# A graph network on one core: low halves unscaled and summed into the high halves' 256 PSUM columns

## The chip, the cores and the metric

The kernel runs on one core of one Trainium2 chip. Its time is the device time of one execution in microseconds (us). The engines are TensorE (PE; its weight loads are listed as PEld), VectorE (DVE), ScalarE (ACT), GpSimd (POOL) and SyncE (SP), which issues most transfers. Each runs its own instruction stream in order, and they meet at semaphores.

## What is computed

A graph of 3125 nodes with 256 features and 50000 edges goes through three layers of three hops each; then comes a residual sum and a layer norm. In short:

```python
norm = dis[src] * dis[dst]              # dis = 1/sqrt(in-degree)
def _tagconv(x, src, dst, norm, W, b):
    out = x @ W[0]
    h = x
    for k in range(1, 4):
        h = segment_sum(norm[:, None] * h[src], dst)
        out = out + h @ W[k]
    return out + b
h = relu(_tagconv(x, ..., W1, b1))
h = relu(_tagconv(h, ..., W2, b2))
out = layernorm(x + _tagconv(h, ..., W3, b3))
```

## The kernel before

**The work.** With g = sqrt(degree) * h and A the matrix of edge counts, a layer is evaluated from its last weight inwards: V3 = (g W3)/degree, V2 = (g W2 + A V3)/degree, V1 = (g W1 + A V2)/degree, and the layer's result is g W0 + A V1. Nodes lie in 25 tiles of 128 (NT = 25; the last has 53 real rows). The items of the program are `("P", L, k, t)`, the product of layer L, weight k and node tile t, and `("T", L, t)`, the transpose of g's tile t into `gT`. `schedule()` writes their order: k = 3 for all 25 tiles, then k = 2, 1, 0, with the transposes and the k = 3 products of layer L+1 placed between the k = 0 tiles of layer L, two tiles behind. The last of them (tile 23, the transpose of 24, tile 24) are placed inside the first k = 2 tile of the next layer, after 3, 10 and 15 of its neighbour products (WQ, WT, WP). Each "P" with k < 3 is called a hop tile here.

**Two halves.** float32 values are held as two float16 numbers, a high half and a low half. `Whl`, `gT` and `V` keep both. The low half is the remainder times SC = 2048, so it needs a sum of its own: a 128x512 PSUM bank holds the high sum in columns 0 to 255 and the scaled low sum in columns 256 to 511. A tile's own product takes two 512-column matmuls of gT's high half against both halves of the weights (L683) and two 256-column matmuls of gT's low half (L685). The neighbour sum takes 24 matmuls of 512 columns, one per source tile, with A's fp8 counts as stationary operand and both halves of V moving (L703), and one of 256 columns for the last source tile, whose 64 rows of high and 64 of low halves share 128 partitions (L708). Its stationary operand `AT` is a float16 copy of those counts, divided by SC in the lower 64 partitions; POOL makes it (L508, L510).

**How a hop tile ends.** For k > 0 four operations alternate between two engines: ACT copies the low columns times 1/degree to `t1` (L597), DVE adds the high columns times SC/degree and writes the sum back to PSUM (L930), ACT rounds it to float16 as the new high half in `V` (L578), DVE subtracts that from PSUM and writes the low half (L908). For k = 0 ACT makes `t1`, DVE makes bias plus `t1` (L935), adds the high columns (L937) and takes the maximum with zero (L941); in the last layer L948, L950 and L954 take the place of these and the layer norm follows. `TensorE` may write a PSUM bank again when DVE has finished with its former tile; five banks rotate (`emptied`).

**The beginning.** About 37 us build degrees, edge lists and the first columns of A. A itself is built from one-hot matrices (DVE L808 and L810, PE L624, ACT L554) in groups, the rest of them inside the first hop stage (L = 0, k = 2), where `trailing()` orders DVE's and ACT's work on groups and on finished tiles. Chained DVE operations on the degrees make the columns of `cst` (L828 to L839), and POOL's scaling of x (L503) waits for the last of them. `largest()` keeps maxima for a check of ranges; if any of 15 lies outside LOW to HIGH, a slow general path runs at the end.

## Time and profile before

| | |
|---|---|
| median of 3 runs | 1498.56 us (1498.47 to 1499.02) |
| the profiled execution: its own time | 1500.34 us |
| its span, first to last instruction | 1498.1 us |
| PE busy, matmuls | 1456.0 us, x7741 |
| DVE busy | 677.7 us, x1608 |
| ACT busy | 360.3 us, x850 |
| POOL busy | 64.0 us, x146 |

The profiled execution lasts 2.2 us longer than its span, and 1.8 us longer than the median of the runs. Busy times are unions, so matmuls that overlap in the array count once. The times of the stages, from the chain of waits: k = 3 of the first layer from about 42 to 71 us, the first hop stage with A's construction to 243 us, and then hop stages of 25 tiles each.

### The profile page before, as it was taken

How to read it: one execution, taken by the hardware profiler on the slowest of the kernel's cores; microseconds unless marked ns; L12 is line 12 of the kernel's file. 1: busy time of each engine (PE TensorE's matmuls, PEld its weight loads, DVE VectorE, ACT ScalarE, POOL GpSimd, SP SyncE). 2: the span in 40 equal slices, each digit the busy share in tenths (PEclk: the TensorE clock that was granted, in tenths of full speed). 3: DMA queues.
4: the chain of work that ended last, by engine and by line, in shares of the span. 5: the costliest groups of instructions: out<-in, count | busy, mean ns of one | idle time of the engine just before them, and what ended most of it. 6: DMA issues, size and time to landing. Idle time of an engine off the chain costs nothing.

```text
span 1498.1 us, 18986 instructions
## 1 busy us (share of the span) xinstructions
PE 1456.0 (97%) x7741; PEld 730.1 (49%) x7741; DVE 677.7 (45%) x1608; ACT 360.3 (24%) x850; POOL 64.0 (4%) x146
## 2 busy tenths in 40 slices
PE   3999999999999999999999999999999999999996
PEld 2555555444455554444444445554444444444443
DVE  7866663333344444333533334445333333335554
ACT  5766663111122222111111112222111111111110
POOL 3300000221000000000000000000000000000000
PEclk9999999999999999999999999999999999999998
DMA  2200000000000000000000000000000000001110
GB/s 72 87 1 1 2 1 1 24 23 11 1 1 1 1 1 0 1 1 1 0 0 1 1 1 1 1 0 1 1 1 0 1 0 1 1 6 48 43 43 22
DMA packets 15470, 15.11 MB, mean 10 GB/s; under 512 B 2362, under 2 KB 15218, under 8 KB 15378
## 3 DMA queue, kind: packets, MB, share of 16 engines
q1 hardware_dynamic: 15138, 13.18, 2.9%
q8 instruction: 63, 1.03, 0.3%
q0 software_dynamic: 240, 0.66, 0.2%
q14 instruction: 29, 0.24, 0.1%
HBM read 10.62 MB, written 3.21 MB: 9 GB/s over the span
## 4 chain that ended last, share of the span: by engine, by line
PE 95%; DVE 4%; issue 1%; ACT 0%; POOL 0%; DMA 0%; DVEq 0%; ACTq 0%
PE pb L703 77%; PE pb L683 8%; PE pb L685 4%; PE pb L624 2%; PE pb L708 2%; PE pb L665 1%; DVE pb L930 1%; DVE V L908 1%; DVE gT L889 0%; PE pb L635 0%; PE pb L646 0%; POOL g L503 0%; DVE Whl L808 0%; DVE Whl L810 0%; ACT t L597 0%
## 5 line engine op out<-in xcount | busy, mean ns | idle before, releaser
L703 PE MATMUL pb<-V,A 128*128 128x512 f16 x5400 | 1226.8, 379 | 0.0
L703 PEld LDWEIGHTS pb<-V,A 128*128 128x128 fp8e4 x5400 | 522.1, 98 | 580.9
L930 DVE SCALAR_TENSOR_TENSOR pb<-pb,cst,t 128x256 f32<-128x256 f32 x225 | 110.2, 490 | 467.3 <-ACT t L597 467.3
L597 ACT ACTIVATE t<-pb,cst 128x256 f32<-128x256 f32 x250 | 118.6, 474 | 691.5 <-PE pb L708 673.7
L683 PE MATMUL pb<-Whl,gT 128*128 128x512 f16 x600 | 210.8, 382 | 0.7 <-DVE gT L889 0.5
L685 PE MATMUL pb<-Whl,gT 128*128 128x256 f16 x600 | 164.6, 274 | 0.0
L908 DVE SCALAR_TENSOR_TENSOR V<-V,pb 128x256 f16<-128x256 f16 (+1 forms) x225 | 94.4, 420 | 92.0 <-ACT V L578 91.8
L578 ACT ACTIVATE V<-pb 128x256 f16<-128x256 f32 (+1 forms) x225 | 86.0, 382 | 140.2 <-DVE pb L930 140.2
L554 ACT ACTIVATE A<-pb 128x500 fp8e4<-128x500 f32 (+1 forms) x157 | 91.3, 585 | 41.7 <-PE pb L624 41.3
L935 DVE SCALAR_TENSOR_TENSOR w<-bb,cst,t 128x256 f32<-128x256 f32 x50 | 24.2, 484 | 168.6 <-ACT t L597 168.6
L921 DVE TENSOR_REDUCE ast<-A 128x1 f32<-128x800 uint8 x100 | 97.6, 976 | 0.0
L683 PEld LDWEIGHTS pb<-Whl,gT 128*128 128x128 f16 x600 | 59.1, 99 | 65.4 <-issue 3.8
L847 DVE TENSOR_REDUCE stat<-V 128x1 f32<-128x256 f16 x225 | 90.7, 412 | 0.3
L624 PE MATMUL pb<-Whl 128*128 128x125 f16 x625 | 63.5, 226 | 6.2 <-ACT A L554 3.7
L624 PEld LDWEIGHTS pb<-Whl 128*128 128x128 f16 x625 | 49.4, 100 | 39.9 <-ACT A L554 6.8
L597 ACT ACTIVATE t<-pb 128x256 f32<-128x256 f32 x50 | 19.2, 384 | 191.5 <-PE pb L708 191.5
L685 PEld LDWEIGHTS pb<-Whl,gT 128*128 128x128 f16 x600 | 59.1, 99 | 7.2
L708 PE MATMUL pb<-V,AT 128*128 128x256 f16 x225 | 61.5, 273 | 0.0
L808 DVE TENSOR_TENSOR Whl<-Whl 128x1024 f16<-128x1024 f16 x79 | 54.2, 686 | 1.4
L810 DVE TENSOR_TENSOR Whl<-Whl 128x1000 f16<-128x1000 f16 x79 | 53.0, 671 | 0.0
L950 DVE SCALAR_TENSOR_TENSOR w<-pb,cst,t 128x256 f32<-128x256 f32 x25 | 12.1, 483 | 55.5 <-ACT t L597 55.5
L708 PEld LDWEIGHTS pb<-V,AT 128*128 128x128 f16 x225 | 22.1, 98 | 27.2 <-DVE V L908 1.0
(118 smaller groups left out, 397.3 us busy)
## 6 DMA issues: line engine op xcount, KB each, us to landing
xr<-in_x SPq DMA_DIRECT2D x48, 128.0 KB, 2.1
out<-g SPq DMA_DIRECT2D x24, 128.0 KB, 1.7
xr<-in_W SPq DMA_DIRECT2D x16, 128.0 KB, 2.0
V<-in_W SPq DMA_DIRECT2D x2, 512.0 KB, 4.1
bb<-in_b SPq DMA_DIRECT2D x3, 128.0 KB, 4.9
xr<-in_x SPq DMA_DIRECT2D x2, 53.0 KB
gT<-in_table,idx POOLq DMA_INDIRECT x5, 2.7
out<-g SPq DMA_DIRECT2D x1, 53.0 KB
```

The costliest lines, as they stand in the source:

```text
L554: act.activation(A8[:, :, gi * GW:gi * GW + n * GD].rearrange("p a (g w) -> p a g w", w=GD), BB[gi % 2][:, 0:n * KEYS].rearrange("p (g a w ...
L578: act.activation(V[vbuf[(L, k)]][0:r, t, 0:F], PB[e][0:r, 0:F], ACT.Copy, scale=1.0 / SC).then_inc(S["s_a2"], 1)
L597: act.activation(t1[:, e % RB, :], lo, ACT.Copy, scale=sc).then_inc(S["s_a1"], 1)
L624: mm = pe.matmul(BB[gi % 2][:, k * KEYS:(k + 1) * KEYS], OB[:, b % NO, vis % BV // VL, :, vis % VL], OK[:, b % NO, vis % BV // VL, :, vis ...
L683: pe.matmul(acc[:, :], gT[:, t, c, 0, :], Whl[:, L, c, k, :], start=(c == 0), stop=False, skip_group_check=True)
L685: mm = pe.matmul(acc[:, F:512], gT[:, t, c, 1, :], Whl[:, L, c, k, 0:F], start=False, stop=(k == 3 and c == 1), skip_group_check=True)
L703: mm = pe.matmul(acc[:, :], A8[:, a, t * P:(t + 1) * P], src[:, a, :], start=False, stop=False, skip_group_check=True)
L708: mm = pe.matmul(acc[:, 0:F], AT[:, t * P:(t + 1) * P], src[:, a, 0:F], start=False, stop=True, skip_group_check=True)
L847: dve.tensor_reduce(stat[:, col:col + 1], ap, axis, ALU.max, apply_absolute_value=True).then_inc(S["s_st"], 1)
L908: dve.scalar_tensor_tensor(lo, vb[0:r, t, 0:F], -SC, hi[0:r, :], ALU.mult, ALU.add).then_inc(S["s_v"], 1)
L921: dve.tensor_reduce(ast[:, nam:nam + 1], A8[:, a_, 800 * i_:800 * i_ + 800].bitcast(U8), AX.X, ALU.max).then_inc(S["s_st"], 1)
L930: dve.scalar_tensor_tensor(hi, hi, cst[:, 1, t:t + 1], t1[:, e % RB, :], ALU.mult, ALU.add).then_inc(S["s_d1"], 1)
```

## The change

SC goes. Low halves are plain remainders (weights are now scaled by SV = 64 and g by SG = 16 in place of 16 and 1, which keeps the remainders away from float16's smallest numbers; LOW becomes 0.25). So all products can be added into the same 256 columns, and every 512-column matmul becomes two of 256 columns with the same stationary operand. A finished tile with k > 0 is read twice from PSUM: ACT writes the high half with the scale 1/degree, DVE writes the low half as PSUM times 1/degree minus the high half. For k = 0 DVE alone reads the sum; ACT's step is gone. The transposed g's low half is a plain subtraction. `AT` is gone: POOL copies the last source tile's counts into the unused 64 partitions of A8's last tile, one operation in place of two. The low halves of the weights of layers 2 and 3 come from one DVE operation each, where POOL made three. The columns of `cst` are 4, not 5, and a column's worth of SC multiplication is gone: two operations less in the chain on the degrees. The order on ACT and DVE has no separate second item ("V") any more.

```diff
-SC = 2048.0
-SV = 16.0
+SG = 16.0
+SV = 64.0
-LOW = 2.0 ** -10
+LOW = 0.25
...
-def trailing(sched, empty, split):
+def trailing(sched, empty):
...
+        t = it[3]
+        gs = [("B", gi) for gi in groups_of(t + 1)]
+        out += gs[:empty] + ([("P", 0, 2, t - 1)] if t else []) + gs[empty:]
+        if t == NT - 1:
+            out.append(it)
...
             for t in range(NT):
                 pool.wait_ge(S["s_ev"], groups_of(t)[-1] + 1)
-                src = A8[0:HALF, NT - 1, t * P:(t + 1) * P]
-                pool.tensor_copy(AT[0:HALF, t * P:(t + 1) * P], src).then_inc(S["s_at"], 1)
-                pool.wait_ge(S["s_at"], 2 * t + 1)
-                pool.tensor_scalar(AT[HALF:P, t * P:(t + 1) * P], AT[0:HALF, t * P:(t + 1) * P], 1.0 / SC, 0.0, ALU.mult,
-                                   ALU.add).then_inc(S["s_at"], 1)
...
+                pool.wait_ge(*((S["s_at"], t) if t else (S["s_gx"], NT)))
+                pool.tensor_copy(A8[HALF:P, NT - 1, t * P:(t + 1) * P],
+                                 A8[0:HALF, NT - 1, t * P:(t + 1) * P]).then_inc(S["s_at"], 1)
...
-            act.wait_ge(S["s_whi"], 1)
-            act.activation(Wsc, hl[:, :, 0:F], ACT.Copy, scale=SC).then_inc(S["s_wp"], 1)
...
+                _, L, k, t = it
+                if k > 0:
+                    act.wait_ge(S["s_ps"], pe_no[(L, k, t)] + 1)
                     r = P if t < NT - 1 else HALF
-                    act.activation(V[vbuf[(L, k)]][0:r, t, 0:F], PB[e][0:r, 0:F], ACT.Copy,
-                                   scale=1.0 / SC).then_inc(S["s_a2"], 1)
+                    act.activation(V[vbuf[(L, k)]][0:r, t, 0:F], PB[pe_no[(L, k, t)]][0:r, 0:F], ACT.Copy,
+                                   scale=cst[0:r, 0, t:t + 1]).then_inc(S["s_a2"], 1)
...
-                act.activation(t1[:, e % RB, :], lo, ACT.Copy, scale=sc).then_inc(S["s_a1"], 1)
...
-                acc = PB[e]
+                acc = PB[e][:, 0:F]
                 for c in range(2):
-                    pe.matmul(acc[:, :], gT[:, t, c, 0, :], Whl[:, L, c, k, :], start=(c == 0), stop=False,
-                              skip_group_check=True)
-                    mm = pe.matmul(acc[:, F:512], gT[:, t, c, 1, :], Whl[:, L, c, k, 0:F], start=False,
+                    for h in range(2):
+                        pe.matmul(acc, gT[:, t, c, 0, :], Whl[:, L, c, k, F * h:F * h + F], start=(c + h == 0), stop=False,
+                                  skip_group_check=True)
+                    mm = pe.matmul(acc, gT[:, t, c, 1, :], Whl[:, L, c, k, 0:F], start=False,
                                    stop=(k == 3 and c == 1), skip_group_check=True)
...
-                            mm = pe.matmul(acc[:, :], A8[:, a, t * P:(t + 1) * P], src[:, a, :], start=False,
-                                           stop=False, skip_group_check=True)
+                            for h in range(2):
+                                pe.matmul(acc, A8[:, a, t * P:(t + 1) * P], src[:, a, F * h:F * h + F], start=False,
+                                          stop=False, skip_group_check=True)
...
-            dl_(dve.tensor_scalar(cst[:, 1, :], cst[:, 0, :], SC, None, ALU.mult))
...
-            dl_(dve.tensor_scalar(cst[:, 3, :], dg[:, 5, :], 2.0 / SV, None, ALU.mult))
-            dve.tensor_scalar(cst[:, 4, :], dg[:, 5, :], 2.0 / (SV * SC), None, ALU.mult).then_inc(S["s_cs"], 1)
+            dve.tensor_scalar(cst[:, 3, :], dg[:, 5, :], 2.0 / (SV * SG), None, ALU.mult).then_inc(S["s_cs"], 1)
...
-                    dve.scalar_tensor_tensor(lo, vb[0:r, t, 0:F], -SC, hi[0:r, :], ALU.mult,
-                                             ALU.add).then_inc(S["s_v"], 1)
+                    dve.scalar_tensor_tensor(lo, acc[0:r, :], cst[0:r, 0, t:t + 1], vb[0:r, t, 0:F], ALU.mult,
+                                             ALU.subtract).then_inc(S["s_v"], 1)
+                    if (L, k) == (0, 2):
+                        largest(v_no[(0, 3, t)], V[vbuf[(0, 3)]][:, t, 0:F], AX.X)
...
-                    dve.wait_ge(S["s_a1"], e + 1)
-                    dve.scalar_tensor_tensor(hi, hi, cst[:, 1, t:t + 1], t1[:, e % RB, :], ALU.mult,
-                                             ALU.add).then_inc(S["s_d1"], 1)
...
+                    dve.tensor_scalar(t2[:, t % 2, :], bb[:, L, :], cst[:, 2, t:t + 1], None,
+                                      ALU.mult).then_inc(S["s_z"], 1)
+                    dve.wait_ge(S["s_z"], L * NT + t + 1)
+                    dve.wait_ge(S["s_ps"], e + 1)
+                    dve.scalar_tensor_tensor(we, acc, 1.0 / SV, t2[:, t % 2, :], ALU.mult,
+                                             ALU.add).then_inc(S["s_d1"], 1)
...
+                    dve.wait_ge(S["s_z"], 2 * NT + t + 1)
+                    dve.wait_ge(S["s_ps"], e + 1)
+                    dve.scalar_tensor_tensor(we, acc, cst[:, 3, t:t + 1], t2[:, t % 2, :], ALU.mult,
                                              ALU.add).then_inc(S["s_d1"], 1)
...
-                    dl_(dve.tensor_tensor(we, we, t2[:, t % 2, :], ALU.add))
```

One hop tile on TensorE, in program order, before the change: the tile's own product, the 24 neighbour matmuls and the last source tile.

```order
L683 MATMUL pb<-Whl,gT 128x512
L685 MATMUL pb<-Whl,gT 128x256
L683 MATMUL pb<-Whl,gT 128x512
L685 MATMUL pb<-Whl,gT 128x256
L703 MATMUL pb<-V,A 128x512 x24
L708 MATMUL pb<-V,AT 128x256
```

The same hop tile in the changed kernel, where L639, L641, L660 and L665 are the lines of L683, L685, L703 and L708.

```order
L639 MATMUL pb<-Whl,gT 128x256 x2
L641 MATMUL pb<-Whl,gT 128x256
L639 MATMUL pb<-Whl,gT 128x256 x2
L641 MATMUL pb<-Whl,gT 128x256
L660 MATMUL pb<-V,A 128x256 x48
L665 MATMUL pb<-V,A 128x256
```

The order of the items on TensorE is as it was; 26 instructions of 512 columns have become 52 of 256.

DVE at the turn from layer L to layer L+1, before the change: the last k = 0 tile (L935, L937, L941), the transposed tile 23 (L889), the k = 3 tiles 22 and 23, and the transposed tile 24.

```order
L935 SCALAR_TENSOR_TENSOR w<-bb,cst,t 128x256
L937 SCALAR_TENSOR_TENSOR w<-pb,w 128x256
L941 TENSOR_SCALAR g<-w 128x256
L889 SCALAR_TENSOR_TENSOR gT<-gT,pb 128x2x128
L847 TENSOR_REDUCE stat<-gT 128x1
L930 SCALAR_TENSOR_TENSOR pb<-pb,cst,t 128x256
L908 SCALAR_TENSOR_TENSOR V<-V,pb 128x256
L847 TENSOR_REDUCE stat<-V 128x1
L930 SCALAR_TENSOR_TENSOR pb<-pb,cst,t 128x256
L908 SCALAR_TENSOR_TENSOR V<-V,pb 128x256
L847 TENSOR_REDUCE stat<-V 128x1
L889 SCALAR_TENSOR_TENSOR gT<-gT,pb 128x2x128
```

DVE at the same place in the changed kernel (L888, L892 and L896 are the k = 0 tile, L844 the transposed tile, L861 the low half, L802 the maxima).

```order
L888 TENSOR_SCALAR w<-bb,cst 128x256
L892 SCALAR_TENSOR_TENSOR w<-pb,w 128x256
L896 TENSOR_SCALAR g<-w 128x256
L844 TENSOR_TENSOR gT<-pb,gT 128x2x128
L802 TENSOR_REDUCE stat<-gT 128x1
L861 SCALAR_TENSOR_TENSOR V<-pb,cst,V 128x256
L802 TENSOR_REDUCE stat<-V 128x1
L861 SCALAR_TENSOR_TENSOR V<-pb,cst,V 128x256
L802 TENSOR_REDUCE stat<-V 128x1
L844 TENSOR_TENSOR gT<-pb,gT 128x2x128
```

Each k = 3 tile has one operation less here and no pause between its two, and L888 no longer needs the tile's sum, so it stands ahead of the wait for TensorE.

## Rows read from the trace of the kernel before

**Rows 1.** The page: busy time by engine, and the chain that ended last.

```profile
PE 1456.0 (97%) x7741; PEld 730.1 (49%) x7741; DVE 677.7 (45%) x1608; ACT 360.3 (24%) x850; POOL 64.0 (4%) x146
...
PE 95%; DVE 4%; issue 1%; ACT 0%; POOL 0%; DMA 0%; DVEq 0%; ACTq 0%
```

**Rows 2.** The chain: start us, length us, what; bodies of hop tiles.

```profile
247.82 5.18 PE pb L703 x24
...
402.24 5.18 PE pb L703 x24
...
421.14 5.18 PE pb L703 x24
...
564.10 5.18 PE pb L703 x24
```

**Rows 3.** Timeline of PE near 480 us: start us, us, engine, line.

```profile
480.62 0.27 PE L708 MATMUL pb<-V,AT 128*128 128x256 f16 x1
480.73 0.38 PE L665 MATMUL pb<-identf,g 128*128 128x128 f32 x2
480.95 0.38 PE L683 MATMUL pb<-Whl,gT 128*128 128x512 f16 x1
```

**Rows 4.** The page's groups: xcount | busy us, mean ns of one | idle before.

```profile
L703 PE MATMUL pb<-V,A 128*128 128x512 f16 x5400 | 1226.8, 379 | 0.0
L703 PEld LDWEIGHTS pb<-V,A 128*128 128x128 fp8e4 x5400 | 522.1, 98 | 580.9
L930 DVE SCALAR_TENSOR_TENSOR pb<-pb,cst,t 128x256 f32<-128x256 f32 x225 | 110.2, 490 | 467.3 <-ACT t L597 467.3
```

**Rows 5.** The chain at the end of the degree work, DVE.

```profile
35.68 0.19 DVE cst L831
...
37.45 0.19 DVE cst L839
```

**Rows 6.** Timeline of PE, last k = 3 tiles of the first layer.

```profile
68.32 0.38 PE L703 MATMUL pb<-V,A 128*128 128x512 f16 x1
...
68.81 0.39 PE L683 MATMUL pb<-Whl,gT 128*128 128x512 f16 x1
...
69.47 0.38 PE L703 MATMUL pb<-V,A 128*128 128x512 f16 x1
...
69.90 0.39 PE L683 MATMUL pb<-Whl,gT 128*128 128x512 f16 x1
```

**Rows 7.** Timeline after the first layer's last k = 3 tile.

```profile
70.76 0.48 ACT L597 ACTIVATE t<-pb,cst 128x256 f32<-128x256 f32 x1 [0.34 <-PE pb L685]
...
72.65 0.69 DVE L808 TENSOR_TENSOR Whl<-Whl 128x1024 f16<-128x1024 f16 x1
...
74.08 0.58 PE L624 MATMUL pb<-Whl 128*128 128x125 f16 x4 [0.96 <-DVE Whl L810]
...
74.46 0.63 PE L703 MATMUL pb<-V,A 128*128 128x512 f16 x1
```

**Rows 8.** Busy us (xcount) of PE, PEld, DVE, ACT, POOL, then granted clock.

```profile
74.00:77.40 3.40, 3.32 (x19) 2.11 (x20) 3.40 (x6) 2.13 (x4) 0.73 (x1) 0.52 0.00 0
```

**Rows 9.** The chain: bodies of hop tiles around the two turns of layers.

```profile
579.14 5.18 PE pb L703 x24
...
1032.02 5.18 PE pb L703 x24
1047.07 5.18 PE pb L703 x24
```

**Rows 10.** The chain after TensorE's last matmul.

```profile
1486.40 0.48 ACT t L597
...
1486.91 0.49 DVE w L950
...
1487.43 0.43 DVE w L954
...
1487.89 0.44 DVE lnb L956
```

More of the change, by code:

```diff
@@ L287, in groups_of @@
     return list(range(last[t] + 1, last[t + 1] + 1)) if t < NT else []
-def trailing(sched, empty, split):
+def trailing(sched, empty):
     out = []
-    held = None
     for it in sched:
-        if it[0] == "T":
+        if it[0] == "T" or it[1:3] != (0, 2):
             out.append(it)
             continue
-        L, k, t = it[1:]
-        if k == 2 and held:
-            out.append(held)
-            held = None
-        if (L, k) == (0, 2):
-            gs = [("B", gi) for gi in groups_of(t + 1)]
-            before = ("P", 0, 2, t - 1), ("V", 0, 2, t - 1)
-            out += (gs[:empty] + ([before[0]] if t else []) + gs[empty:split] + ([before[1]] if t else [])
-                    + gs[split:])
-            if t == NT - 1:
-                out += [it, ("V",) + it[1:]]
-            continue
-        out.append(it)
-        if held:
-            out.append(held)
-        held = ("V",) + it[1:] if k > 0 else None
-        if held and (L, k) != (0, 3):
-            out.append(held)
-            held = None
+        t = it[3]
[3 more added lines that the diff above has]
+            out.append(it)
     return out
@@ L333, in bass_tag_gnn_layernorm @@
     p_of = {e: key for key, e in pe_no.items()}
+    d_no = {key: n for n, key in enumerate(key for key in pe_no if key[1] == 0)}
     vbuf = {(L, k): (L + 3 - k) % 2 for L in range(3) for k in (3, 2, 1)}
@@ L560, in _ @@
             act.wait_ge(S["s_cs"], 1)
-            for it in trailing(SCHED, 0, 2):
+            for it in trailing(SCHED, 0):
                 if it[0] == "B":
@@ L569, in _ @@
                     act.activation(gT[:, t, :, 0, :], TB[j % 2][:, 0:F].rearrange("p (c m) -> p c m", c=2),
-                                   ACT.Copy, scale=1.0 / SC).then_inc(S["s_th"], 1)
+                                   ACT.Copy).then_inc(S["s_th"], 1)
                     continue
-                what, L, k, t = it
-                e = pe_no[(L, k, t)]
-                if what == "V":
-                    v = v_no[(L, k, t)]
-                    act.wait_ge(S["s_d1"], e + 1)
+                _, L, k, t = it
+                if k > 0:
+                    act.wait_ge(S["s_ps"], pe_no[(L, k, t)] + 1)
                     r = P if t < NT - 1 else HALF
-                    act.activation(V[vbuf[(L, k)]][0:r, t, 0:F], PB[e][0:r, 0:F], ACT.Copy,
-                                   scale=1.0 / SC).then_inc(S["s_a2"], 1)
+                    act.activation(V[vbuf[(L, k)]][0:r, t, 0:F], PB[pe_no[(L, k, t)]][0:r, 0:F], ACT.Copy,
+                                   scale=cst[0:r, 0, t:t + 1]).then_inc(S["s_a2"], 1)
                     if (L, k) == (0, 1) and t < 16:
@@ L585, in _ @@
                                        scale=SV).then_inc(S["s_wi"], 1)
[L586 to L598 removed]
+                elif L == 2:
                     act.wait_ge(S["s_ln"], t + 1)
@@ L611, in emptied @@
                 else:
-                    pe.wait_ge(S["s_d1"], pe_no[was] + 1)
+                    pe.wait_ge(S["s_d1"], d_no[was] + 1)
             def build(gi):
@@ L651, in _ @@
                 build(gi)
-            pe.wait_ge(S["s_wp"], 2)
+            pe.wait_ge(S["s_wp"], 1)
             def work(it, within={}):
@@ L702, in work @@
                         if a < NT - 1:
-                            mm = pe.matmul(acc[:, :], A8[:, a, t * P:(t + 1) * P], src[:, a, :], start=False,
-                                           stop=False, skip_group_check=True)
+                            for h in range(2):
+                                pe.matmul(acc, A8[:, a, t * P:(t + 1) * P], src[:, a, F * h:F * h + F], start=False,
+                                          stop=False, skip_group_check=True)
                             continue
                         if (L, k) == (0, 2):
-                            pe.wait_ge(S["s_at"], 2 * t + 2)
-                        mm = pe.matmul(acc[:, 0:F], AT[:, t * P:(t + 1) * P], src[:, a, 0:F], start=False,
+                            pe.wait_ge(S["s_at"], t + 1)
+                        mm = pe.matmul(acc, A8[:, a, t * P:(t + 1) * P], src[:, a, 0:F], start=False,
                                        stop=True, skip_group_check=True)
@@ L879, in verdict_ranges @@
                                   ALU.mult).then_inc(S["s_ck"], 1)
-            for it in trailing(SCHED, 4, 6):
+            for it in trailing(SCHED, 4):
                 if it[0] == "B":
@@ L894, in _ @@
                     continue
-                what, L, k, t = it
+                _, L, k, t = it
                 e = pe_no[(L, k, t)]
-                hi = PB[e][:, 0:F]
+                acc = PB[e][:, 0:F]
                 we = w[:, t % 2, :]
@@ L901, in _ @@
                     vb = V[vbuf[(L, k)]]
-                if what == "V":
                     dve.wait_ge(S["s_a2"], v + 1)
```

68 lines of the change are left out of this document (20 added, 48 removed).

## The prediction

> **What bounds the kernel now.** I read the page first: PE is busy for 97% of the span and makes up 95% of the chain that ended last, DVE and ACT are busy 45% and 24% [rows 1]. So the question is what a hop tile's stream of matmuls costs, and at which few places TensorE waits for the ends of tiles. The chain in order of time shows how regular the stream is. In the plain hop stages one tile body follows the next from 247.82 to 402.24 us, 26 tiles apart, which is 5.939 us a tile; in the k = 0 stages that carry transposes and k = 3 products as well, 21 tiles lie between 421.14 and 564.10 us, 6.808 us each [rows 2]. No wait stands between them. A DVE or ACT operation saved inside these stages buys nothing; what TensorE itself does there counts in full.
>
> From these two periods follows the price of one matmul, start to start. Call it x for 512 columns and y for 256. A plain tile is 26x + 3y (24 L703 and two L683; two L685 and one L708). The richer tile adds two transposes and one more product, 2 transposes + 2x + 2y = 6.808 - 5.939 = 0.868 us. Two transposes take 0.22 us, as much as two 256-column matmuls [rows 3], so 2x + 4y = 0.868. Solved: x = 215.8 ns, y = 109.2 ns. The check is the body itself, 24x = 5.18 us [rows 2]. The mean of 379 ns in the page's group is the time from start to result of one matmul, most of it overlapped, and must not be used as its price [rows 4].
>
> **What the change adds.** A pair of 256-column matmuls costs 2y = 218.4 ns where one of 512 cost 215.8: 2.5 ns more, a fixed part paid once more. Pairs: 5400 for L703 [rows 4] and 600 for L683 (300 products, two each), 6000 in all. 6000 x 2.53 ns = 15.1 us, in every stage, all of it on TensorE, which has no slack. From the rounding of the rows the pair's price is good to 0.1 ns, 0.6 us in the sum.
>
> This takes a step that no row shows: a 256-column matmul behind another 256-column one with the same weights. The weight load takes 98 ns [rows 4] and must fit into a slot of 109. In the trace a load does hide in such a slot once per L708 and L685, with a 512-column matmul next; now it must do so 55 times in a row. Bounds: if nothing extra is paid for the second matmul, 0; if the fixed part is paid, 15; if the load does not hide, much more (the second rival). I take 15.1, since y was measured with a load in its slot.
>
> **What it saves.** Only the places where TensorE waits for a tile's end.
> - Degrees: two of the chained DVE operations go, each about 0.2 us with its hand-over, and POOL and TensorE wait behind the last [rows 5]: -0.4 us.
> - The last k = 3 tiles of the first layer: TensorE stands from 68.32 + 0.216 to 68.81 and from 69.47 + 0.216 to 69.90 [rows 6], 0.27 and 0.21 us, because DVE with three operations a tile frees banks late. With two operations DVE has slack (its own period was the same 1.08 us as TensorE's): -0.5 us.
> - After them, DVE starts the one-hots for which TensorE waits until 74.08 only when the last tile is finished: 72.65 - 70.76 = 1.89 us of four operations in turn [rows 7]. Now two: ACT's with a column as scale, like L597, 0.48 us, and DVE's at L930's 0.49 [rows 4], with hand-overs 1.02 us. -0.9 us.
> - Right behind, from 74.0 to 77.4 us, the granted clock is 0.52, the lower level of 1.2 GHz [rows 8], after TensorE had mostly stood for some three microseconds; a 512-column matmul then takes 0.63 us [rows 7]. With 3.32 us of matmuls in it, that costs up to 1.66 us. Since the waits ahead of it shrink by a third or more, it may not happen. Ends 0 and -1.6; I take -0.8.
> - The two turns of layers. Between the bodies at 564.10 and 579.14 stand 58 matmuls of x and 16 of y (two k = 3 products inside the tile and one before it, the transposes): 14.27 us, where 15.04 passed; at the second turn 15.05 (1032.02 to 1047.07) [rows 2, 9]. TensorE stands 0.78 us each time, for transposed tiles and V tiles that DVE delivers late. There DVE loses about 0.9 us on the k = 0 tile (ACT's step and L935 are out of the way) and some 0.8 on each of the k = 3 tiles 22 and 23, far more than the waits. -1.6 us. What would be late next is the k = 3 tile 24 behind its transpose; by my count its low half of gT comes about 0.1 us ahead of need.
> - The end: from 1486.40 to 1487.89 run ACT, L950 and L954 [rows 10], 1.49 us; one DVE operation of 0.49 remains. -1.0 us.
>
> Edits at no cost: POOL's one copy for two operations and no weight work; one more DVE operation of some 0.42 us in 16 tiles of the first layer's k = 1 stage and the moved maxima (DVE is below half busy there, under a 6 us tile); ACT's first-layer weight pass, done long before TensorE reads weights. If that cover went, each would cost its own length, under 0.5 us a tile. Nothing is queued behind the new waits for TensorE on DVE that was not behind the wait for ACT before: L888 now even stands ahead.
>
> **Sum.** +15.1 - 0.4 - 0.5 - 0.9 - 0.8 - 1.6 - 1.0 = +9.9 us. On the profiled execution, 1500.3 us (span 1498.1 and 2.2 around it), that gives 1510.2; the median of the runs is 1.8 lower, so **1508.5 us**. With the savings between 4.4 and 6.0 and the pairs at 15.1 +- 0.6 the case spans 1507.0 to 1509.9.
>
> **The rivals.**
> - *The pair costs nothing more: faster.* If the second matmul of a pair, whose weights are already there, follows the first without the fixed part, x stands for a pair and only the savings remain: 1498.6 - 5.2 = 1493.4 us. It decides from below 0.35 ns a pair on ((5.2 - 3.0)/6000); up to 1.4 ns a pair it would look like no change. For it: the weights do repeat. Against: the fixed part is the same 2.5 ns for 128 float32 columns, 256 and 512 (x - 2y), so it hangs on the matmul and not on new weights. 5%.
> - *Weight loads or sums into columns written 109 ns before become the bound: much slower.* A load of 98 ns leaves 11 ns. If the slot became 98 + 20, say, 55 slots a tile would cost 0.5 us each, 110 us over 225 tiles; every 1 ns is 12 us. Against: y itself holds a load, and L685 adds into columns that the L683 ahead of it wrote some 109 ns earlier, at no visible cost. 7%.
> - The Trainium skill, "TensorE: Matmul & The Clock Gate", section "Back-to-back issue gap", speaks against halving: it gives sustained streams of load and matmul 81 ns at 128 columns and 131 ns at 512, a large fixed part for each pair. Read between these, 256 columns would take some 98 ns, a pair 196 for 131, an estimate of 6000 x 65 ns = 390 us more. Here the trace disagrees: 512 columns take 215.8 ns, not 131. It is this rival's far end, and I leave it 1 of the 7%.
> - *The savings don't come: +15.* A new order lets another operation be late (transposed tile 24 above all), or the lower clock comes at another place, or the two-operation ends are not on the chain where I think. Price: 5 us, 1513.7; with a second stretch of lower clock 1515. 8%.
>
> **How the numbers follow.** Forecast 77%, its near neighbours 3% (a pair price between 0.35 and 1.4 ns, which ends as no change), rivals 5, 7 and 8%. A change of 0.2% is 3.0 us, about what a measurement of this kernel can tell. Faster 0.05, same 0.03, slower 0.92. The range reaches from 1504 (a pair at 1.8 ns) to 1514 (no savings), and leaves out some 15%.
>
> **What would show it.** In the changed profile: 13,741 matmuls; the plain tile's body, now 48 matmuls, 5.24 us, and the tile period 55y = 6.00 us (+0.065); bodies at the turns 14.4 us apart; no wait of TensorE on DVE after the k = 3 stage's banks; the last matmul's end followed by one DVE operation before the layer norm; DVE's busy time down by some 100 us and ACT's by some 120, at no gain of their own. It would be wrong if the period of the plain stages stayed at 5.94, or rose beyond 6.05 us.

## The result and the profile after

The changed kernel takes **1510.82 us**, the median of 3 runs (1510.66 to 1511.25), where the kernel before took 1498.56: 12.3 us more, a ratio of 1.0082 (95% interval 1.0059 to 1.0104). Its profiled execution took 1510.66 us, with a span of 1508.9.

The page of the changed kernel, with the lines that answer to [rows 1] and [rows 4]. L660 is the old L703, L861 the DVE operation that is left of L930 and L908, L545 the ACT operation that is left of L597 and L578.

```profile
PE 1467.7 (97%) x13741; PEld 1316.0 (87%) x13741; DVE 569.1 (38%) x1372; ACT 253.1 (17%) x549; POOL 34.1 (2%) x73
...
PE 97%; DVE 2%; issue 1%; POOL 0%; DMA 0%; ACT 0%; DVEq 0%; ACTq 0%
...
L660 PE MATMUL pb<-V,A 128*128 128x256 f16 x10800 | 1239.9, 273 | 0.0
L660 PEld LDWEIGHTS pb<-V,A 128*128 128x128 fp8e4 x10800 | 1050.2, 98 | 119.3
L861 DVE SCALAR_TENSOR_TENSOR V<-pb,cst,V 128x256 f16<-128x256 f32 (+1 forms) x225 | 108.4, 482 | 603.8 <-ACT V L545 603.7
L545 ACT ACTIVATE V<-pb,cst 128x256 f16<-128x256 f32 (+1 forms) x225 | 106.7, 474 | 741.2 <-PE pb L665 714.6
```

6000 matmuls have come, 13,741 in place of 7,741, and each brings a weight load with it (730 us of loads have become 1316). DVE works 109 us less and ACT 107 us less, but DVE's share of the chain that ended last only falls from 4% to 2%. That is the whole trade: a little more on the engine that bounds the kernel, a lot less on two that do not.

The chain of the changed kernel (start us, length us, what), which answers to [rows 2] and [rows 9]: the first and last of 27 bodies in the plain stages, and the bodies on either side of the first turn of layers.

```profile
11.69 7.96 issue
247.72 5.24 PE pb L660 x48
...
403.83 5.24 PE pb L660 x48
...
567.36 5.24 PE pb L660 x48
581.87 5.24 PE pb L660 x48
```

26 tiles lie between 247.72 and 403.83: 6.004 us each, where 5.939 stood. That is 0.065 us for 26 pairs, **2.50 ns a pair**; 6000 pairs are 15.0 us. The turn takes 14.51 us in place of 15.04. The first row is one that I had not looked at: a stretch of 7.96 us in the prologue was 6.11 before. The timelines of both kernels there, first before (start, length, engine and line, in brackets how long the engine had waited and for whom):

```profile
12.18 1.18 POOL L496 DMA_INDIRECT gT<-in_table,idx  x1 [6.06 <-DVE idx L745]
12.61 2.29 DVE L749 SCALAR_TENSOR_TENSOR Whl<-V 128x2048 f16<-128x2048 f32 x1 [0.73 <-ACT V L535]
13.67 2.06 POOL L496 DMA_INDIRECT gT<-in_table,idx  x1 [0.30 <-issue]
15.26 0.29 DVE L770 TENSOR_TENSOR g<-gT,thr 128x128 f32<-128x128 int32 x1 [0.36 <-DMA gT<-in_table,idx]
```

And after:

```profile
11.81 2.29 DVE L706 SCALAR_TENSOR_TENSOR Whl<-V,Whl 128x2048 f16<-128x2048 f32 x1
12.19 2.96 POOL L478 DMA_INDIRECT gT<-in_table,idx  x1 [6.06 <-DVE idx L702]
15.46 0.95 POOL L478 DMA_INDIRECT gT<-in_table,idx  x1 [0.30 <-issue]
...
17.07 0.29 DVE L727 TENSOR_TENSOR g<-gT,thr 128x128 f32<-128x128 int32 x1 [2.97 <-DMA gT<-in_table,idx]
```

DVE makes the first layer's low halves in one operation of 2.29 us. Before, it had to wait 0.73 us for ACT's pass (L535), and POOL began the first gather's issue 0.43 us ahead of it and had it done in 1.18 us; the second issue, which began beside the DVE operation, took 2.06 and ended 0.83 us after it. The change removes ACT's pass; DVE starts at 11.81, ahead of the gather, and now the first issue takes 2.96 us and ends 1.05 us after DVE does. The table's first rows reach DVE at 17.07 instead of 15.26, **1.8 us later**, and the whole prologue moves with them.

The places where TensorE waited, in the changed kernel. The first stage's end, which answers to [rows 6] and [rows 7]:

```profile
70.95 0.38 PE L660 MATMUL pb<-V,A 128*128 128x256 f16 x2
71.16 0.47 ACT L545 ACTIVATE V<-pb,cst 64x256 f16<-64x256 f32 x1 [0.40 <-PE pb L641]
...
71.66 0.48 DVE L861 SCALAR_TENSOR_TENSOR V<-pb,cst,V 64x256 f16<-64x256 f32 x1 [0.39 <-ACT V L545]
72.17 0.69 DVE L765 TENSOR_TENSOR Whl<-Whl 128x1024 f16<-128x1024 f16 x1
...
74.78 0.40 PE L579 MATMUL pb<-Whl 128*128 128x125 f16 x4 [0.35 <-DVE Whl L767]
```

From ACT's start to DVE's one-hots 1.01 us pass, where 1.89 did. The half-speed stretch is not there; the windows' row for the stretch of [rows 8] says (the figure before the 0.03 is the granted clock):

```profile
74.00:77.40 3.40, 3.05 (x36) 2.69 (x35) 3.40 (x8) 2.67 (x6) 1.30 (x1) 1.00 0.03 5
```

At the turn, DVE's transposed tile 24 (L844) and the product that needs it:

```profile
577.13 1.26 PE L660 MATMUL pb<-V,A 128*128 128x256 f16 x10
577.75 0.42 DVE L844 TENSOR_TENSOR gT<-pb,gT 128x256 f16<-128x256 f32 x1 [0.84 <-ACT gT L538]
...
578.32 0.38 PE L639 MATMUL pb<-Whl,gT 128*128 128x256 f16 x2
```

Ten matmuls at 109.1 ns from 577.13 end at 578.22; L639 starts at 578.32. By this TensorE still stands 0.10 us at each turn.

The end, which answers to [rows 10]:

```profile
1498.31 0.48 DVE L906 SCALAR_TENSOR_TENSOR w<-pb,cst,w 128x256 f32<-128x256 f32 x1 [2.79 <-PE pb L665]
1498.83 0.43 DVE L910 BATCH_NORM_STATS2 lnb<-w 128x6 f32<-128x256 f32 x1
```

0.52 us where 1.49 stood.

**Where the 10.8 us between the two spans are** (1498.1 to 1508.9), in us:

| place | predicted | found | from |
|---|---|---|---|
| 6000 pairs | +15.1 | +15.0 | tile period 5.939 to 6.004 |
| gather behind DVE | not priced | +1.8 | first data at 15.26, now 17.07 |
| degrees | -0.4 | -0.4 | two operations gone: 3.08 us of chain, now 2.67 |
| last k = 3 tiles of the first stage | -0.5 | -1.1 | bank waits 0.49; the rest below |
| one-hots behind them | -0.9 | -0.9 | 1.89 to 1.01 |
| half-speed stretch | -0.8 | -1.0 | granted clock 0.52, now 1.00; a wait of 0.35 that comes with full speed taken off |
| two turns | -1.6 | -1.4 | TensorE stood 0.78 us at each, now 0.10 |
| end | -1.0 | -1.0 | 1.49 to 0.52 |
| sum | +9.9 | +11.0 | |

The places come to 0.2 us more than the spans differ; I could not place that. The rest in the fourth line is an estimate. In both traces a lone 256-column matmul is recorded at 0.42 us until about 46.6 us and at 0.27 from there on, as at half speed and at full speed, though the views give the granted clock as 1.00 on both sides. TensorE starts its products 1.4 us later in the changed kernel, so fewer of them are slow ones. The same delay is thus a loss in the prologue and a small gain behind it. The size of that gain is an accident of the two executions: over the eleven traces of this case the matmuls become short anywhere between 44.7 and 47.9 us, and each us of that is worth about half a us. Nor does the table say that the half-speed stretch went because of the change; experiment 7 has a trace on that.

### The profile page after: what moved, and what is told of

Same layout as the page of the kernel before. It is cut to its first block, busy times and chain, and to the rows that moved or that the text cites. A ratio compares the mean times of both kernels' runs of the same rounds, so it can differ in the third digit from the quotient of the medians.

```text
span 1508.9 us, 30155 instructions
## 1 busy us (share of the span) xinstructions
PE 1467.7 (97%) x13741; PEld 1316.0 (87%) x13741; DVE 569.1 (38%) x1372; ACT 253.1 (17%) x549; POOL 34.1 (2%) x73
## 2 busy tenths in 40 slices
DMA packets 15511, 15.83 MB, mean 10 GB/s; under 512 B 2362, under 2 KB 15218, under 8 KB 15378
## 4 chain that ended last, share of the span: by engine, by line
PE 97%; DVE 2%; issue 1%; POOL 0%; DMA 0%; ACT 0%; DVEq 0%; ACTq 0%
PE pb L660 78%; PE pb L639 9%; PE pb L641 4%; PE pb L579 2%; PE pb L665 2%; PE pb L620 1%; PE pb L590 0%; DVE Whl L765 0%; DVE Whl L767 0%; PE pb L601 0%; POOL g L485 0%; DVE V L731 0%; DVE V L700 0%; DMA t<-in_heads 0%; DVE t L696 0%
## 5 line engine op out<-in xcount | busy, mean ns | idle before, releaser
L660 PE MATMUL pb<-V,A 128*128 128x256 f16 x10800 | 1239.9, 273 | 0.0
L660 PEld LDWEIGHTS pb<-V,A 128*128 128x128 fp8e4 x10800 | 1050.2, 98 | 119.3
L861 DVE SCALAR_TENSOR_TENSOR V<-pb,cst,V 128x256 f16<-128x256 f32 (+1 forms) x225 | 108.4, 482 | 603.8 <-ACT V L545 603.7
L545 ACT ACTIVATE V<-pb,cst 128x256 f16<-128x256 f32 (+1 forms) x225 | 106.7, 474 | 741.2 <-PE pb L665 714.6
L639 PE MATMUL pb<-Whl,gT 128*128 128x256 f16 x1200 | 211.5, 274 | 0.0
L641 PE MATMUL pb<-Whl,gT 128*128 128x256 f16 x600 | 164.1, 274 | 0.0
L639 PEld LDWEIGHTS pb<-Whl,gT 128*128 128x128 f16 x1200 | 117.7, 98 | 13.5 <-issue 0.4
L892 DVE SCALAR_TENSOR_TENSOR w<-pb,w 128x256 f32<-128x256 f32 x50 | 21.2, 425 | 223.7 <-PE pb L665 223.7
L802 DVE TENSOR_REDUCE stat<-V 128x1 f32<-128x256 f16 x225 | 92.1, 409 | 0.3
L538 ACT ACTIVATE gT<-pb 128x256 f16<-128x256 f32 x75 | 28.8, 384 | 292.0 <-PE pb L620 292.0
L641 PEld LDWEIGHTS pb<-Whl,gT 128*128 128x128 f16 x600 | 58.9, 98 | 7.0
L665 PE MATMUL pb<-V,A 128*128 128x256 f16 x225 | 61.3, 273 | 0.0
L906 DVE SCALAR_TENSOR_TENSOR w<-pb,cst,w 128x256 f32<-128x256 f32 x25 | 12.1, 484 | 68.5 <-PE pb L665 68.5
L844 DVE TENSOR_TENSOR gT<-pb,gT 128x256 f16<-128x256 f32 x75 | 31.3, 418 | 3.2 <-ACT gT L538 3.2
L802 DVE TENSOR_REDUCE stat<-gT 128x1 f32<-128x256 f16 x75 | 30.7, 409 | 0.0
L620 PE MATMUL pb<-identf,g 128*128 128x128 f32 x150 | 29.9, 283 | 0.6 <-POOL g L485 0.6
```

Source lines behind the costliest of these rows:

```text
L545: act.activation(V[vbuf[(L, k)]][0:r, t, 0:F], PB[pe_no[(L, k, t)]][0:r, 0:F], ACT.Copy, scale=cst[0:r, 0, t:t + 1]).then_inc(S["s_a2"], 1)
L639: pe.matmul(acc, gT[:, t, c, 0, :], Whl[:, L, c, k, F * h:F * h + F], start=(c + h == 0), stop=False, skip_group_check=True)
L641: mm = pe.matmul(acc, gT[:, t, c, 1, :], Whl[:, L, c, k, 0:F], start=False, stop=(k == 3 and c == 1), skip_group_check=True)
L660: pe.matmul(acc, A8[:, a, t * P:(t + 1) * P], src[:, a, F * h:F * h + F], start=False, stop=False, skip_group_check=True)
L665: mm = pe.matmul(acc, A8[:, a, t * P:(t + 1) * P], src[:, a, 0:F], start=False, stop=True, skip_group_check=True)
L802: dve.tensor_reduce(stat[:, col:col + 1], ap, axis, ALU.max, apply_absolute_value=True).then_inc(S["s_st"], 1)
```

## The experiments

Each experiment was timed beside the kernel before on its own chip; the first four shared one chip (before: 1499.67 us, 7 runs, 1498.41 to 1500.69), the next four another (before: 1499.75, 16 runs, 1497.63 to 1501.77). The letters of the theories are those of the expectations: A is that every matmul has a fixed part of 2.5 ns, which halving pays a second time, and that the rest of the change only shows where TensorE waited.

### 1. Only the matmul cut in two, into separate halves

Into the kernel before. If summing into columns just written has a price (B), this has it not.

```
-                            mm = pe.matmul(acc[:, :], A8[:, a, t * P:(t + 1) * P], src[:, a, :], start=False,
-                                           stop=False, skip_group_check=True)
+                            for h in range(2):
+                                pe.matmul(acc[:, F * h:F * h + F], A8[:, a, t * P:(t + 1) * P],
+                                          src[:, a, F * h:F * h + F], start=False, stop=False, skip_group_check=True)
```

> The kernel before, with only the neighbour matmuls (L703) cut into two of 256 columns, the high half into columns 0 to 255 and the low half into 256 to 511; scales, ends of tiles and everything else as before. Theory A (a fixed part of 2.5 ns is paid for each matmul, whatever it writes): 5400 more matmuls, +13.5 us, 1512 us, and a plain tile period of 5.939 + 24 x 0.0025 = 6.000 us. Rival B (the cost comes from adding two matmuls in a row into the same 256 columns): no change, 1498.6 us, period 5.94.

Measured: 1511.73 us (1511.61 to 1512.47, 4 runs), ratio 1.0082 (1.0066 to 1.0099). The chain of this kernel, first and last of 27 bodies:

```profile
247.52 5.24 PE pb L704 x48
...
403.50 5.24 PE pb L704 x48
```

156 us for 26 tiles, 5.999 each: 0.060 us more for 24 pairs, 2.50 ns a pair, to separate columns as to the same. The cut alone, without the rescaling or the shorter ends, costs 12.1 us here; 5400 pairs at 2.5 ns are 13.5, which the interval (9.9 to 14.8 us) holds. B is out.

### 2. High halves first, then low halves

In the changed kernel, outside the first hop stage: the two matmuls that share their weights no longer follow each other.

```
+                    apart = (L, k) != (0, 2)
...
-                            for h in range(2):
+                            for h in range(1 if apart else 2):
                                 pe.matmul(acc, A8[:, a, t * P:(t + 1) * P], src[:, a, F * h:F * h + F], start=False,
                                           stop=False, skip_group_check=True)
                             continue
+                        for a2 in range(NT - 1 if apart else 0):
+                            pe.matmul(acc, A8[:, a2, t * P:(t + 1) * P], src[:, a2, F:512], start=False,
+                                      stop=False, skip_group_check=True)
```

> The changed kernel, with the 24 matmuls of the high halves first and then the 24 of the low halves in all hop stages but the first, so that neighbouring matmuls have different weights. Theory A (2.5 ns hang on the matmul): no change, 1510.8 us, period 6.00 us. Rival C (a repeated weight load makes the second matmul of a pair cheaper or dearer than one with new weights): the period moves; a cheaper repeat of 1 ns would show as +4.8 us (200 tiles x 24).

Measured: 1512.56 us (1511.79 to 1512.85, 4 runs), ratio 1.0085 (1.0068 to 1.0102). Its chain splits the body in its two halves:

```profile
430.11 2.62 PE pb L661 x24
432.73 2.62 PE pb L665 x24
```

Twice 2.62 is the same 5.24: whether the weights change from one matmul to the next or repeat makes no difference. The span grew by 2.0 us over the changed kernel's, and for another reason. The k = 3 products and transposes are placed after so many values of a; with one matmul per value ahead of them in place of two, they come earlier than DVE can deliver. In this kernel TensorE waits for the transposed tile 24 longer than 0.10 us:

```profile
577.52 0.38 PE L639 MATMUL pb<-Whl,gT 128*128 128x256 f16 x2 [0.48 <-DVE gT L848]
```

I count 0.9 us of standing per turn here, 1.6 us more at the two turns together; most of the other 0.4 lies where the matmuls become short, 0.7 us later in this execution. The place where prediction and trace put the next late operation is thus real: as soon as the need comes earlier, the wait there grows.

### 3. The first layer's ACT pass put back

To hold DVE's low-half operation back as before, for the 1.8 us of the prologue.

```
+            act.wait_ge(S["s_whi"], 1)
+            act.activation(Wsc, hl[:, :, 0:F], ACT.Copy, scale=1.0).then_inc(S["s_whi"], 1)
...
-            dve.wait_ge(S["s_whi"], 1)
+            dve.wait_ge(S["s_whi"], 2)
```

> The changed kernel, with the removed ACT pass over the first layer's weights put back (its result is not used) and DVE's low-half operation waiting for it as before, so that this operation of 2.29 us starts at about 12.6 us in place of 11.8. Theory D (it overlaps the work of GpSimd that issues the first gather, which took 2.96 us in place of 1.18, and holds the gather up): the first gather lands 1.8 us earlier, DVE's wait for it ends near 15.3 us, -1.8 us, 1509.0 us. Rival E (the gather's landing varies by itself): no change, 1510.8 us.

Measured: 1509.74 us (1508.72 to 1510.33, 4 runs), ratio 1.0066 (1.0049 to 1.0082). It settles nothing, as its trace shows:

```profile
9.18 1.91 ACT L507 ACTIVATE V<-Whl 128x2048 f32<-128x2048 f16 x1
...
11.84 2.29 DVE L709 SCALAR_TENSOR_TENSOR Whl<-V,Whl 128x2048 f16<-128x2048 f32 x1
12.22 2.96 POOL L479 DMA_INDIRECT gT<-in_table,idx  x1 [6.06 <-DVE idx L705]
```

In this execution the weights had landed 1.4 us earlier, the pass was over by 11.09, and DVE was ahead of the gather again. A delay by a pass whose own start depends on a DMA holds nothing in place. It may also be one reason why the kernel before varies from run to run (1497.6 to 1501.9 over all its later runs here), since whether the gather gets its gap hangs on when the weights land; that was not tried by itself. Experiment 5 does it with an order.

### 4. The changed kernel's matmuls, the old kernel's four operations

ACT scales the sum, DVE scales it too and takes the larger of the two (equal numbers, so the values stay), then ACT and DVE make the halves as before; in the k = 0 tiles of the first two layers each scales it by half and DVE adds.

```
+                if what == "P" and k > 0 and split4:
+                    dve.wait_ge(S["s_a1"], f + 1)
+                    dve.scalar_tensor_tensor(acc, acc, cst[:, 0, t:t + 1], t1[:, f % RB, :], ALU.mult,
+                                             ALU.add if both else ALU.max).then_inc(S["s_d1"], 1)
+                    continue
...
+                        dve.scalar_tensor_tensor(lo, vb[0:r, t, 0:F], -1.0, acc[0:r, :], ALU.mult,
+                                                 ALU.add).then_inc(S["s_v"], 1)
```

> The changed kernel's matmuls, all of 256 columns, with the ends of tiles of the kernel before: for k > 0 ACT copies to t1, DVE combines and writes back, ACT makes the high half, DVE the low; for k = 0 ACT, DVE, DVE and, in the last layer, one DVE operation more. The sum lies in one half only, so the combining step takes the larger of two equal values. Theory F (the ends are worth what the waits of TensorE show): about 0.6 us at the first layer's last k = 3 tiles, 0.9 behind them, 1.4 to 1.5 at the turns and 1.0 at the end come back: +4 us, 1514.8 us. Rival G (the savings came from elsewhere or were none): within 1 us of 1510.8.

Measured: 1514.47 us (1513.84 to 1515.96, 4 runs), ratio 1.0103 (1.0086 to 1.0119). The busy time of this kernel's engines, and TensorE's waits (in total us, times, longest):

```profile
PE 1468.6 (97%) x13741; PEld 1315.3 (87%) x13741; DVE 681.7 (45%) x1622; ACT 358.1 (24%) x849; POOL 33.9 (2%) x73
```

```profile
PE pb L625 <- ACT A L549: 3.7, 3, 2.4
...
PE pb L690 <- DVE gT L898: 0.4, 2, 0.2
```

In the changed kernel the first of these waits is 2.8 and the second is not there. The span is 3.1 us above the changed kernel's, the median 3.7 (from another chip); the four places of the table that hang on the ends (bank waits, one-hots, turns, end) make 0.5 + 0.9 + 1.4 + 1.0 = 3.8. DVE's 113 us and ACT's 105 us of added work elsewhere cost nothing.

### 5. The gather issued first

In the changed kernel, DVE's low-half operation waits until POOL has issued the first gather.

```
+                    if q == 0:
+                        pool.memset(want[:, 3:4], 0.0).then_inc(S["s_gi"], 1)
...
+            dve.wait_ge(S["s_gi"], 1)
             dve.scalar_tensor_tensor(hl[:, :, F:512], Wraw, SV, hl[:, :, 0:F], ALU.mult, ALU.subtract).then_inc(S["s_wp"], 1)
```

> The changed kernel, with DVE's low-half operation on the first layer's weights (2.29 us) held back until GpSimd has issued the first of its five gathers. In the run before, the operation still began at 11.84 us, since the weights had come 1.4 us earlier, so that nothing was told apart. Theory D (an operation of DVE that runs while GpSimd issues a gather holds the issue up until it ends): the first issue takes 1.2 us in place of 2.96, the second 2.0 or more, DVE starts on the first gather's data near 15.7 us in place of 17.1, -1.4 us: some 1509.4. Rival E: the first issue still takes about 3 us, and the time stays at 1510.8.

Measured: 1509.80 us (1509.46 to 1510.07, 5 runs), ratio 1.0068 (1.0054 to 1.0081). The prologue of this kernel:

```profile
12.20 1.19 POOL L478 DMA_INDIRECT gT<-in_table,idx  x1 [6.06 <-DVE idx L704]
...
13.62 2.29 DVE L709 SCALAR_TENSOR_TENSOR Whl<-V,Whl 128x2048 f16<-128x2048 f32 x1 [1.73 <-POOL want L481]
13.69 3.05 POOL L478 DMA_INDIRECT gT<-in_table,idx  x1 [0.20 <-issue]
15.83 0.28 DVE L730 TENSOR_TENSOR g<-gT,thr 128x128 f32<-128x128 int32 x1
```

The first issue is back to 1.19 us, and now the second, which falls beside the DVE operation, takes 3.05 and ends 0.83 us after it. DVE starts on the table 1.2 us earlier (17.07 to 15.83). The second gather is now the late one, and of the 1.2 us only 0.8 reach TensorE's products (they start at 42.18 in place of 42.97). The span fell by 1.3 us (1508.9 to 1507.6); the other 0.5 come from the matmuls, which become short at 44.7 us in this execution and at 46.6 in the other. The medians differ by 1.0 us, from two chips. So the gather's issue is held while this DVE operation runs, and the term that the prediction left out is shown by putting the cause back.

### 6. Both widths, each where it is worth it

512 columns and four operations for most tiles; 256 columns and two operations for the first stage, the last k = 3 tiles and the last k = 0 tile of each layer. Rescaling and the gather's order are those of experiment 5.

```
+def wide(L, k, t):
+    return not ((L, k) == (0, 3) or k == 3 and t >= 22 or k == 0 and t == NT - 1)
...
```

> Unscaled low halves as in the changed kernel, so that a tile may be done in either way: 512-column matmuls and an end in four operations (k > 0) for most tiles, 256-column matmuls and the short end only where TensorE waits: all k = 3 tiles of the first layer, k = 3 tiles 22 to 24 of the others, and tile 24 of each k = 0 stage. The low-half operation on the first weights waits for the first gather's issue. If theories A and F hold, the 2.5 ns are paid 0.14 thousand times, 0.4 us, and the savings stay: 0.5 (degrees), 0.6 and 0.9 (first k = 3 stage), 1.4 (turns), 1.0 (end): 1498.6 - 4.0 = 1494.6 us, and up to 1 us less from the gather. Rival H (the savings need short ends throughout, or the two kinds of tile disturb each other): 1497 us or more.

Measured: **1494.81 us** (1494.59 to 1496.15, 6 runs) beside 1499.75, ratio 0.9970 (0.9958 to 0.9982). Page and chain of this kernel:

```profile
PE 1453.9 (97%) x7881; PEld 743.9 (50%) x7881; DVE 672.3 (45%) x1590; ACT 349.7 (23%) x815; POOL 34.5 (2%) x74
```

```profile
246.14 5.18 PE pb L713 x24
...
406.50 5.18 PE pb L713 x24
...
562.42 5.24 PE pb L716 x48
576.87 5.18 PE pb L713 x24
```

The period is back at 5.94 us, with 140 pairs paid in place of 6000, 0.35 us, and the short ends stand at the few places where TensorE waits for an end: 14.45 us at the turn. It is faster than both kernels: 0.3% below the one before, and the interval excludes 1.

### 7. Unscaled low halves with 512 columns and four operations throughout

Experiment 6 with 512 columns and four operations everywhere, and the gather's order as in the changed kernel. Against the kernel before it has the rescaling, the shorter degrees, the other small edits and the late gather.

```
 def wide(L, k, t):
-    return not ((L, k) == (0, 3) or k == 3 and t >= 22 or k == 0 and t == NT - 1)
+    return True
...
```

> Unscaled low halves and the changed kernel's other edits (degrees, GpSimd's single copy, weights on DVE), but 512-column matmuls and long ends for all tiles. It parts what the rescaling alone does from the matmuls' split and the ends. If A and F hold: the kernel before less 0.5 us for the degrees, 1498 to 1499 us, with a plain tile period of 5.94 us. A rival (the other edits matter): more than 1 us off that.

Measured: 1499.38 us (1498.80 to 1501.36, 10 runs), ratio 1.0001 (0.9992 to 1.0010). All these edits together can't be told from nothing (-1.2 to +1.5 us). By the table they should come to about +0.8 (gather 1.8, degrees -0.4, fewer slow matmuls -0.6), which that interval holds; so the gather's 1.8 us are shown by traces and not by these medians. Experiment 6 lies 4.6 us below this kernel on the same chip, and the few tiles with short ends and the gather's order are all that parts the two; the 12 us of loss are the width's.

This trace also has the waits ahead of the half-speed stretch as they were before the change. TensorE waits 1.07 us for ACT and 0.97 for DVE here, in the kernel before 1.07 and 0.96 (the second stands in [rows 7]). The PE timeline there, and the windows' row (the granted clock is the 1.00 ahead of 0.00):

```profile
74.26 0.40 PE L625 MATMUL pb<-Whl 128*128 128x125 f16 x4 [0.97 <-DVE Whl L821]
```

```profile
74.00:77.40 3.40, 2.80 (x26) 1.94 (x27) 3.40 (x7) 2.33 (x5) 0.87 (x1) 1.00 0.00 0
```

The same waits, and full speed behind them. The traces of experiments 1 and 4, with the long ends too, also stand at 1.00 there. Of eleven traces only that of the kernel before has the stretch. The stretch thus can be absent with the long ends too. It came in that one execution and not in the others, and its going is not shown to be an effect of the change.

### 8. 128 columns in one stage

In the changed kernel, the hop stage L = 1, k = 1 in matmuls of 128 columns. A slot is then 56 ns and a weight load takes 98, so if loads can be a bound (I) it must show here.

```
-                            for h in range(2):
-                                pe.matmul(acc, A8[:, a, t * P:(t + 1) * P], src[:, a, F * h:F * h + F], start=False,
-                                          stop=False, skip_group_check=True)
+                            C = 128 if (L, k) == (1, 1) else F
+                            for h in range(512 // C):
+                                pe.matmul(acc[:, C * h % F:C * h % F + C], A8[:, a, t * P:(t + 1) * P],
+                                          src[:, a, C * h:C * h + C], start=False, stop=False, skip_group_check=True)
```

> The changed kernel, with the neighbour matmuls of one hop stage (second layer, k = 1) cut again, into four of 128 columns; 1200 matmuls become 2400 there. Theory A (only the fixed 2.5 ns): body of a tile 5.24 + 0.12 = 5.36 us, +3.1 us, 1513.9. Rival I (a weight load becomes the bound once the matmul is shorter than it, 98 ns each): body 96 x 98 = 9.4 us, +104 us. In between (matmuls of 125 columns stood 59 ns apart in A's construction): body 5.7 us, +12 us, 1522.

Measured: 1514.23 us (1512.86 to 1514.46, 4 runs), ratio 1.0095 (1.0079 to 1.0110). The chain, from the last body of 256 columns into the stage, and its last:

```profile
720.55 5.24 PE pb L661 x48
726.55 5.36 PE pb L661 x96
...
873.53 5.36 PE pb L661 x96
```

146.98 us for 24 tiles, 6.124 each: 0.120 us more than 6.004 for 48 further matmuls, 2.50 ns each again. The loads are no bound even at this spacing: in 130 us of this stage (730 to 860 us) there are 2190 of them, which at 98 ns each would be 215 us one after the other, so they overlap each other too.

### 9. The DVE operation in pieces

Experiment 6, but with no order: the low halves in eight DVE operations of 256 columns, free to start at once.

```
-            dve.wait_ge(S["s_gi"], 1)
-            dve.scalar_tensor_tensor(hl[:, :, F:512], Wraw, SV, hl[:, :, 0:F], ALU.mult, ALU.subtract).then_inc(S["s_wp"], 1)
+            for m in range(8):
+                last = dve.scalar_tensor_tensor(hl[:, m, F:512], Wraw[:, m, :], SV, hl[:, m, 0:F], ALU.mult, ALU.subtract)
+                if m == 7:
+                    last.then_inc(S["s_wp"], 1)
```

> The kernel of the run mixed, with the low-half operation on the first weights (2.29 us) no longer held back but cut into eight of some 0.29 us. In gather_first and mixed the hold-up had only moved to the second gather's issue, 3.05 us in place of 0.95, which ends 0.85 us after DVE's operation. Theory D2 (the issue is held for the length of one DVE operation): with short pieces each issue takes at most 0.3 to 0.6 us longer, DVE starts on the first gather's data near 15.5 us, the second gather is no longer late, and the time falls by 0.5 to 1 us, to 1494.0. Rival (the issue is held until DVE pauses, however short its operations): the first issue takes about 3 us again, DVE starts at 17.1, and the time is 1495.5 or more.

Measured: 1494.81 us (1494.27 to 1495.91, 5 runs) beside 1500.30 (9 runs), ratio 0.9966 (0.9952 to 0.9980). Its prologue:

```profile
11.80 2.77 DVE L761 SCALAR_TENSOR_TENSOR Whl<-V,Whl 128x256 f16<-128x256 f32 x8
12.18 1.43 POOL L504 DMA_INDIRECT gT<-in_table,idx  x1 [6.07 <-DVE idx L756]
13.92 1.14 POOL L504 DMA_INDIRECT gT<-in_table,idx  x1 [0.31 <-issue]
15.36 0.95 POOL L504 DMA_INDIRECT gT<-in_table,idx  x1 [0.30 <-issue]
15.50 0.29 DVE L784 TENSOR_TENSOR g<-gT,thr 128x128 f32<-128x128 int32 x1 [0.93 <-DMA gT<-in_table,idx]
```

The same work, 2.77 us of it beside the same two issues, now holds them by 0.2 us each (1.43 and 1.14 against 1.19 and 0.95) and not by two. So it is the length of one DVE operation that holds the issue, not DVE's being busy. The span is 0.8 us shorter than in experiment 6; 0.4 of it is there when TensorE starts its products (41.71 in place of 42.15), and the rest comes with matmuls that become short over a us earlier. The medians, from two chips, are equal, so on the time the two cannot be told apart.

## Why the prediction held, and where it was off

**The pairs**, the term on which it stood, are right: 15.1 predicted, 15.0 found, 2.50 ns each. The row that carried it was the tile period, not the mean of one matmul. Experiments 1, 2 and 8 bear out the step that "no row shows": a 256-column matmul behind another costs its 109.1 ns, to the same or other columns, with the same or other weights, and the load hides. Both rivals on this price are out, the one that makes the kernel faster and the one that makes it much slower.

**The savings** are right place by place to 0.2 us in the two traces compared, but for the k = 3 tiles of the first stage, -1.1 for -0.5, and there the extra is the slow matmuls of the start and not the banks. The half-speed stretch is right in number only: the prediction let it hang on the waits ahead of it, and experiment 7 has those waits without it. Experiment 4 puts the old ends back and loses 3.1 to 3.7 us of the 3.8 counted. Of the third rival, its first half is true in small: the transposed tile 24, named there, delays TensorE by 0.10 us a turn and does not come 0.1 us ahead of need, which is why the turns gave 1.4 and not 1.6.

**A term was missing.** The prediction put "ACT's first-layer weight pass, done long before TensorE reads weights" among the edits at no cost. The reader of the weights was not the one to ask. The pass kept a long DVE operation away from POOL's gather; without it the gather is issued late and +1.8 us follow. The wait that DVE lost was a cover for another engine. Experiment 5 brings the table's first rows 1.2 us earlier by the trace, of which 0.8 reach the products.

**The step from the profiled execution to the median** was also wrong. The sum was made against 1500.3 us, and gave 1510.2; the changed kernel's profiled execution took 1510.66, 0.5 more. I then took off 1.8 because the median of before lay that much lower. But the half-speed stretch of [rows 8] belongs to that profiled execution: ten other traces, three of them with the same long ends, don't have it. Its saving was counted in the sum and, with the 1.8, a second time. Against medians it falls away: 15.0 + 1.8 - 0.4 - 1.1 - 0.9 - 1.4 - 1.0 = 12.0, where 12.3 was measured. That the clock sets the 1.8 us apart is only argued. Of 32 later runs of the kernel before, the four with the mean granted clock of that execution, 0.996, took 1500.1 to 1501.9 us, the others 1497.6 to 1501.3, which fits but does not show it; no run here holds the clock fixed.

The gather (1.8) and the stretch (0.8) together are 2.6 us, more than the 2.3 between 1508.5 and 1510.82. The slow matmuls of the start took 0.6 of them back, which the prediction did not have and which another execution would have given differently, and some 0.3 are not placed. That the miss is no larger is in part luck.

## What to carry to other kernels

Price the engine that bounds the kernel by its period, start to start, and multiply: 2.5 ns looks like nothing and is 1% of the time when it is paid 6000 times, while 216 us saved on two idle engines buy only what lies in a few waits. A trade between such a cost in every tile and a saving in a few can be made tile by tile; here that turned +12 us into -5. Before an operation or a wait is called free, see what the other engines do in that gap, and when a term rests on one profiled execution, ask whether the median has it too.

## What the runs showed of the hardware

A matmul's fixed part at full clock is 2.5 ns at 512, 256 and 128 columns, with a weight load recorded at 98 ns ahead of each one and slots down to 56 ns: 215.8, 109.1 and 55.8 ns start to start (the last from bodies of 96 in 5.36 us). The Trainium skill, "TensorE: Matmul & The Clock Gate", section "Back-to-back issue gap", gives 131 ns and 81 ns for sustained streams of load and matmul at 512 and 128 columns; these runs show neither. The same page of the Trainium skill, section "Wait — 56ns, not 53.3ns?", gives 55.6 and 215.7 ns for 128 and 512, and with that the runs agree.

The clock behind the same waits is not the same in each execution: with waits of 1.07 and 0.97 us ahead of it TensorE ran on at a granted clock of 1.00 in one trace and, with 1.07 and 0.96, at 0.52 in another, 1.0 us of time between the two; and at the start its matmuls became short at 44.7 to 47.9 us in eleven traces. A difference of a us between two traces is not yet an effect of an edit.

The issue of an indirect DMA on POOL takes 1.18 to 1.19 us alone the first time and 0.95 us later on, and 2.96 to 3.05 us where it begins beside or just behind the start of one DVE operation of 2.29 us, and then ends 0.8 to 1.05 us after that operation; one that began 0.43 us ahead of it was not held. Beside eight short ones of 2.77 us in all it takes 1.43. The Trainium skill, "GPSIMD Engine Reference", section "Key points", says that POOL shares its SBUF interfaces with VectorE, with contention where a DVE instruction has two inputs in SBUF. This one has two, and the runs agree; whether one with a single input would hold the issue was not tried.
